# Turning sixteen row tiles of the first stage by VectorE and DRAM transfers in place of TensorE

## What is computed

```python
x = x + tanh(g_xattn[0]) * L0_xattn(layernorm(x), ctx, ...)   # part 0: 16 heads, latent attention
x = x + tanh(g_ffn[0])   * L0_ffn(layernorm(x), ...)          # part 1: routed LoRA experts
x = x + tanh(g_xattn[1]) * L1_xattn(layernorm(x), ctx, ...)   # part 2: causal attention
x = x + tanh(g_ffn[1])   * L1_ffn(layernorm(x), ...)          # part 3: low-rank experts
```

## Time and profile before

| | |
|---|---|
| median of 3 runs | 1376.98 us |
| the profiled execution | 1372.65 us, span 1370.8 us |
| TensorE matmul / weight load | busy 98% / 80% |
| VectorE, ScalarE, GpSimd | busy 68%, 38%, 31% |
| first stage | about the first 450 us of the span |
| transfers of the core's 16 DMA engines | mean 101 GB/s |
| TensorE's granted clock | 0.997 of full, over the span |

### The profile page before, as it was taken

The page is one execution under the profiler, slowest core; times in us unless marked ns, Lnnn a source line. Parts: engine busy times, 40 slices in busy tenths (PEclk is TensorE's granted clock), DMA queues, the critical chain, the costliest instruction groups (busy, mean ns, idle before and its releaser), DMA issues.

```text
span 1370.8 us, 20464 instructions
## 1 busy us (share of the span) xinstructions
PE 1345.0 (98%) x7596; PEld 1091.3 (80%) x7596; DVE 929.3 (68%) x1787; ACT 518.2 (38%) x1569; POOL 421.5 (31%) x463
## 2 busy tenths in 40 slices
PE   7999999999999999999999999999999999999999
PEld 5788888888888788878887888788876788887777
DVE  5665675666674878786678667766988877745533
ACT  3545445444464322231123111311127777822220
POOL 3222333233254352111121111114428865630000
PEclk9999999999999999999999999999999999999999
DMA  7553434433444222210121012112334131144431
GB/s 268 189 173 114 143 117 130 131 124 119 145 152 116 88 77 87 87 42 16 53 79 53 29 39 91 37 49 75 100 107 139 29 119 63 52 136 152 139 123 54
DMA packets 108615, 138.35 MB, mean 101 GB/s; under 512 B 12876, under 2 KB 66252, under 8 KB 108516
## 3 DMA queue, kind: packets, MB, share of 16 engines
q1 hardware_dynamic: 108516, 137.05, 31.7%
HBM read 97.15 MB, written 39.85 MB: 100 GB/s over the span
## 4 chain that ended last, share of the span: by engine, by line
PE 86%; DVE 8%; DMA 2%; ACT 1%; issue 1%; POOL 1%; SPq 1%; DVEq 0%; ACTq 0%
PE bank L118 82%; PE bank L121 4%; DVE XR L140 1%; DVE AH L130 1%; DVE STG L130 1%; DVE AH L127 1%; DVE st L152 1%; DMA XR<-scr 1%; SPq L170 1%; DVE PYZ L164 1%; DVE XR L137 1%; ACT Pb L124 0%; DMA pscr<-PYZ 0%; ACT STG L124 0%; DVE sm L146 0%
## 5 line engine op out<-in xcount | busy, mean ns | idle before, releaser
L118 PE MATMUL bank<-XT,AR 128*128 128x512 f32 x1152 | 280.6, 393 | 0.3 <-DVE AR L130 0.2
L118 PE MATMUL bank<-AR 128*128 128x512 f32 x1056 | 260.5, 396 | 0.9 <-DVE PTV L127 0.7
L118 PEld LDWEIGHTS bank<-XT,AR 128*128 128x128 f32 x1152 | 214.2, 188 | 48.7 <-issue 1.7
L124 ACT ACTIVATE STG<-bank,b1c 128x512 f32<-128x512 f32 x128 | 88.3, 690 | 387.6 <-PE bank L118 321.4
L118 PEld LDWEIGHTS bank<-AR 128*128 128x128 f32 x1056 | 193.8, 188 | 45.7 <-DVE AR L130 1.5
L118 PE MATMUL bank<-AR,CT 128*128 128x512 f32 x768 | 192.8, 394 | 0.0
L118 PE MATMUL bank<-AR,AH 128*128 128x512 f32 x768 | 185.9, 390 | 0.0
L127 DVE CAST AH<-STG 128x512 fp32r<-128x512 f32 x192 | 95.0, 495 | 111.8 <-PE bank L118 96.6
L118 PEld LDWEIGHTS bank<-AR,AH 128*128 128x128 f32 x768 | 143.6, 188 | 30.7 <-issue 1.1
L118 PEld LDWEIGHTS bank<-AR,CT 128*128 128x128 f32 x768 | 140.0, 188 | 27.2 <-issue 0.4
L127 POOL CAST BA<-STG 128x256 fp32r<-128x256 f32 x64 | 31.5, 492 | 396.0 <-PE bank L118 243.1
(11 more groups left out here) (139 smaller groups left out, 1834.4 us busy)
## 6 DMA issues: line engine op xcount, KB each, us to landing
XR<-scr SPq DMA_DIRECT2D x64, 256.0 KB, 2.9
pscr<-PYZ SPq DMA_DIRECT2D x30, 512.0 KB, 2.9
PYZ<-pscr SPq DMA_DIRECT2D x120, 128.0 KB, 2.9
XR<-in_x_dram SPq DMA_DIRECT2D x32, 256.0 KB, 3.7
scr<-XR SPq DMA_DIRECT2D x32, 256.0 KB, 2.1
STG<-in_Wq_dram SPq DMA_DIRECT2D x8, 512.0 KB, 5.5
STG<-in_WoT_dram SPq DMA_DIRECT2D x8, 512.0 KB, 6.1
STG<-in_W1L_dram SPq DMA_DIRECT2D x16, 256.0 KB, 2.8
```

The lines of the kernel that those rows point to most:

```text
L118: return self.e.matmul(o, w, x, start=start, stop=stop, skip_group_check=True) if self.e else Nothing()
L124: return self.e.activation(o, x, func, **kw) if self.e else Nothing()
```

## The change

The sixteen row tiles (0, 1), (0, 2), (0, 3) and (1, 0), each with four `tb`, are turned as in the second stage. TensorE's `ln_turn` in the first stage goes (only the four tiles of block 0 keep it). VectorE adds `ln_blocks` after `ln_norm` in p 3 to 6, into a buffer `LNY` of its own that takes an unused gap. SP adds `ln_store` and `ln_back` (one store and four loads) after `p_load`. A step later, in p 4 to 7, ScalarE and VectorE run `ln_split` (high and low part, read from `XR`) at the place where `ln_turn` stood.

```diff
-            sb("gap", [128, 608], F32, st1)
+            LNY = sb("LNY", [128, 608], F32, st1)
...
         def by_blocks(ph, m):
-            return (ph, m) in ((1, 1), (1, 2), (1, 3), (2, 0))
+            return (ph, m) in ((0, 1), (0, 2), (0, 3), (1, 0), (1, 1), (1, 2), (1, 3), (2, 0))
+
+        def in_stage1(ph, m):
+            return ph == 0 or (ph, m) == (1, 0)
 
         def ly(ph, m):
-            return xr_ap("tail", 1, (m - 1) % 4, 0)
+            return LNY[:, 0:512] if in_stage1(ph, m) else xr_ap("tail", 1, (m - 1) % 4, 0)
 
         def ly_free(ph, m):
+            if in_stage1(ph, m):
+                if (ph, m) == (0, 1):
+                    return t_ly.sem, 0
+                return t_ly[0, m - 1 if m else 3, 3]
             return xr_free("tail", 1, (m - 1) % 4, 0)
...
@@ tensor
-                if u < NU and 3 <= p <= 6:
-                    ln_turn(*after1(m), p - 3, ring4.next())
@@ scalar
-                if u < NU and 3 <= p <= 6:
-                    ln_turn(*after1(m), p - 3)
+                if u < NU and 4 <= p <= 7:
+                    ln_split(*after1(m), p - 4)
@@ vector
                 if u < NU and 3 <= p <= 6:
                     ln_norm(*after1(m), p - 3)
+                    ln_blocks(*after1(m), p - 3)
...
-                if u < NU and 3 <= p <= 6:
-                    ln_turn(*after1(m), p - 3)
+                if u < NU and 4 <= p <= 7:
+                    ln_split(*after1(m), p - 4)
@@ sync
                 if 2 <= u < NU:
                     p_load(u - 2)
+                if u < NU and 3 <= p <= 6:
+                    ln_store(*after1(m), p - 3)
+                    ln_back(*after1(m), p - 3)
```

## The result

The changed kernel takes 1379.49 us (median of 20 runs, 1376.96 to 1384.11) against 1376.04 (20 runs) of the kernel before on the same chip: ratio 1.0025, 95% interval 1.0018 to 1.0032, so 3.4 us slower (2.5 to 4.4). Measured again on another chip it gave 1379.84 (10 runs) against 1376.45, ratio 1.0025 (1.0012 to 1.0038). The forecast was 1377.9, +0.9. The 3.4 us lie above the 0.2% that the prediction had set as its line for a change. The profiled executions stand further apart, 1378.01 against 1372.65 us: the one of before was the fastest that was seen of that kernel.

The account below looks back on a forecast made before the run. TensorE was taken to bound most first-stage steps, VectorE some or nearly so. Block terms -1.2, +0.4, +0.4 and +1.3 gave +0.9 us, 1377.9 us on the median; own range 1375 to 1380.5, widened to 1373 to 1382.5.

Parts of the forecast that it names:

- TensorE, -7.0: First stage: 16 tiles' transposes at 0.44 us each leave TensorE's list, 7.0 us in all.
- B = 0.78: VectorE's block transpose ahead of the row maxima delays the exps by 0.78 us per tile step, bounds 0.6 to 1.0.
- Block 0, -1.2: Steps 3 to 6: 1.76 us gained from four transposes, 0.55 lost waiting for a later weight load.
- Rival B: Block 0, steps 4 to 6: the round trip makes weight loads late, up to +5.6 us, middle 1381; chance 0.15.
- Blocks 1 and 2, +0.4 each: Tile steps of both blocks: TensorE's 1.76 us saving is taken back by VectorE, +0.4 us each.
- Step 9, nothing: First-stage step in which no tile is turned; the prediction had no term for it.
- Block 3, +1.3: Steps 27 to 30, GpSimd splitting the next stage's weights: +1.3 us, the middle of +0.5 and +2.1.
- the better end: Block 3 if `ln_norm` and GpSimd pass each other: step 29 costs nothing, step 30 about -0.15; +0.5 us.
- SP and DMA, nothing: Later blocks: the tile's store and loads on SP and a `kv_load` 3.8 us later cost nothing.
- Behind the first stage, nothing: Kernel parts after the first stage: the prediction counted no cost there.
- A: First stage: VectorE's added work stays hidden, all 7.0 us come off, 1370.0 us; chance 0.19 with a half-way case.
- C: Nine bound steps: GpSimd blocks VectorE's tile split and `ln_norm`, +4.8 us, 1382.7 us; chance 0.08.

Follow-up runs that it names:

- e6: Changed kernel with the row tile's normalization and block transpose behind the row maxima, and VectorE's `PT` behind the block transposes: 1368.23 us, ratio 0.9940.
- e9: Kernel before, tiles turned by TensorE, with normalization moved behind the row maxima and `PT` behind the block transposes: 1371.32 us, ratio 0.9964.
- e8: Changed kernel without VectorE's block transpose of the sixteen tiles, transfers still made: 1374.93 us, ratio 0.9990.
- e1: Changed kernel with `ln_norm` and `ln_blocks` moved behind the row maxima: 1374.70 us, ratio 0.9988.
- e10: Changed kernel with GpSimd's low parts of the next stage's weights cut to 8 of 512 columns in steps 28 to 31: 1378.08 us, ratio 1.0011.
- e11: Changed kernel measured again, unaltered, on another chip: 1379.84 us, ratio 1.0025.
- e12: Changed kernel with 64 calls of unused 4-column matmuls added at the start of TensorE's list (128 in the trace): 1379.38 us, ratio 1.0022.
- e3: Changed kernel with the four tiles of (1, 0) turned by TensorE as before: 1376.43 us, ratio 1.0005.
- e7: Changed kernel without the store and four loads of each of the sixteen tiles, block transposes still made: 1379.37 us, ratio 1.0025.
- e4: Changed kernel with only the tiles of (0, 1) turned the new way, the twelve others by TensorE: 1378.13 us, ratio 1.0014.
- e5: Changed kernel with VectorE's `PT` moved behind the block transposes in every step: 1381.37 us, ratio 1.0036.

## Why the prediction was right, and where it was off

- *TensorE, -7.0*: right. 64 transposes fewer; where nothing else binds, a tile step takes 11.64 in place of 12.09 us (e6 against e9).
- *B = 0.78 ahead of the maxima*: right in place and size. Four step lengths came within 0.1 us. e8 gives 4.8 us for the sixteen, less than eleven bound steps at 0.78 (8.6): without the transposes the round trip of the probabilities takes over in some steps.
- *Block 0, -1.2*: -1.74 in the profile pair. SP's delay was right (3.70 against 3.8), but the sum let Wqr land after 4.4 us and it took 3.3, so it was there when TensorE came. The sum also let TensorE come 0.44 us earlier, though more than one turn had been taken off ahead of it; it came 0.83 earlier. Those two errors cancel only in part, and the result is better than forecast by luck of one landing: four other profiles with the same tiles (e1, e10, e11, e12) have one step of 16.7 to 16.8 us, a wait of 0.3. Rival B was near, and did not happen.
- *Blocks 1 and 2, +0.4 each*: +0.38 and +0.44. The waits were partly elsewhere than forecast: TensorE stood 0.95 and 0.40 us before `pv1` in steps 11 and 12 (forecast 1.2 and 1.1) and not at all in 13 and 14 (0.4 and 0.3). In those two it is the weight load that waits, 0.17 for the exps and 0.24 for `CT` in step 13 and 0.21 for `CT` in step 14, which the transposes had covered.
- *Step 9, nothing*: left out. It took 0.49 us more, and 0.52 in e11. The prediction had no term for the round trip of the probabilities, which closes in nearly a step's length; one profile of the kernel before can't tell whether its steps 9 are ever long too.
- *Block 3, +1.3 (0.5 to 2.1)*: the mis-sized term. e3 gives 2.8 us, the two profiles 3.5 and 2.3. In the first profile the pass in step 29 came as the better end had it (`ln_norm` 0.81), but step 30 was hit: I had only let one operation be stretched, where here the normalization, and after the transpose the negation, lay beside 5.74 us of GpSimd, and the trace of before already had both in step 30, at 0.81 and 0.54; and I had priced no fall of the clock (the matmuls behind it took 0.62 + 0.61 + 0.27 = 1.5 us more than those of step 29). The Trainium skill's sentence on the ports ("SBUF — State Buffer", Terms: one instruction holds the shared pair to its end, the other engine is blocked) agrees with these rows and with e10, where 0.51 us returns; I had cited it and still let it act once per step.
- *SP and DMA, nothing*: right (e7).
- *Behind the first stage, nothing*: off, a term put at nothing. The wait in the last part grew by 0.7 in the profile, with the clock's fall behind it: 2.2 us of the profiles' difference arise there.
- *Rivals*: A (the work is hidden) is wrong in the given order and comes half true once both locks are open. C named the right resource but the wrong place: `XT<-XR` took 680 to 683 ns in the first stage (eight tiles; the eight that the trace names `AR<-XR` took 682 on average); GpSimd hit `ln_norm` and the negation in block 3.
- *The sum*, +0.9: +3.4, inside the range 1373 to 1382.5 and at the edge of the forecast's own (-2.0 to +3.5). With all its bad ends together that one would have reached +5.1 (0.9 + 2.2 + 0.8 + 1.2). The prediction gave 0.54 to a change within 0.2% and 0.27 to one slower than that; the second came. The two engines cancel in blocks 0 to 2, as forecast; the excess is seen in block 3, step 9 and the last part. How much of it the change brings each time is not settled, since e4 loses 2.5 us in block 3 without the change there. The rule weighed beside A, a 128x128 transpose belongs to TensorE ("VectorE: DVE Perf Modes", Rules for kernel authors, in the Trainium skill), holds in the given order, and the measurement goes against it once both moves are made in VectorE's list (0.9940 against 0.9964).

## What to carry to other kernels

Ask of a step not only how much slack the second engine has, but how many loops close at nearly the step's length: here VectorE's order ahead of the maxima and the round trip of the probabilities, and neither opened alone gave the full gain (0.9988 and 1.0036, but 0.9940 together). The same change cost 3.4 us in one order of VectorE's list and gained 3.3 in another, so settle the order first, then move work between engines. A stall of TensorE near 2 us can bring a fall of its clock behind it, 1.5 us more here in step 30; it is a risk to weigh, since not every such stall brought one (next section).

## What the runs showed of the hardware that was not expected

- TensorE's granted clock fell from 1.00 to 0.50 behind idle stretches of 1.90 and 1.94 us; behind 1.27 us in the kernel before it did not. But the length of the idle stretch does not settle it. In the last part it fell behind 2.07 to 2.49 us in e1, e3, e5, e6, e11 and e12, and stayed at 1.00 behind 2.23, 2.33 and 2.49 us in e7, e10 and e8. Near 1040 us every kernel has an idle stretch of 1.43 us; the clock fell there in e4, e6, e10 and e11 and in no other profile.
- A 16 KB packet of the instruction queue among eight load issues of SP goes with 0.8 to 1.8 us more for them, and where it falls follows the count of TensorE's matmuls from the start: taking 64 away some 900 us earlier moved it onto these issues. So a change can cost time in code that it does not touch.
- A `tensor_scalar` on 128x4 elements took 1.06 us beside GpSimd's work, 0.17 without; on 128x512, 1.55 against 0.51.
